# Maxima of a masked attention over pieces of 512, 512, 512 and 65 columns instead of four of about 401

## The reference

```python
scores = scale * einsum("bhqd,bhkd->bhqk", q, k)      # 2048 x 1601 a head
scores = where(mask, -large, scores)                  # int32 mask, 2048 x 1601
out    = softmax(scores) @ v                          # then the output projection
```

## Time and profile before

| | before |
|---|---|
| median of 3 runs | 3051.54 us (3050.11 to 3053.46) |
| the profiled execution's own time | 3052.74 us |
| its span | 3051.0 us |
| PE busy | 2817.6 us, 92% |
| DVE busy | 2171.2 us, 71% |
| ACT busy | 1824.3 us, 60% |
| POOL busy | 542.7 us, 18% |
| TensorE clock granted, mean over the span | 0.952 |

### The profile page before, as it was taken

How to read it: one execution, slowest core, us unless ns; L and a number is a source line. 1 busy time by engine, 2 the same in 40 slices (tenths; PEclk the granted TensorE clock), 3 DMA queues, 4 the chain that set the end, 5 groups by cost and what they waited for, 6 DMA issues and landing times. The chain is left out here.

```text
span 3051.0 us, 93944 instructions
## 1 busy us (share of the span) xinstructions
PE 2817.6 (92%) x39186; PEld 1046.2 (34%) x39187; DVE 2171.2 (71%) x6062; ACT 1824.3 (60%) x2158; POOL 542.7 (18%) x760
## 2 busy tenths in 40 slices
PE   4999999999999999967999998999999999899997
PEld 2522222522222222233222224652222222256664
DVE  7688986587878887565899993158888888652114
ACT  2388878436666666734588886234777777831222
POOL 0188870110000000001222113111000000002330
PEclk7899999979999999978899999997999999999999
DMA  3345541301110001102111112020111111111112
GB/s 98 111 130 131 135 111 35 118 18 25 25 26 25 17 24 26 36 20 76 33 47 43 42 45 83 1 74 23 39 52 52 52 53 32 35 58 62 44 43 86
DMA packets 120407, 166.79 MB, mean 55 GB/s; under 512 B 38227, under 2 KB 89310, under 8 KB 119984
## 3 DMA queue, kind: packets, MB, share of 16 engines
q1 hardware_dynamic: 102192, 117.21, 14.3%
q0 software_dynamic: 12320, 43.02, 4.6%
q10 hardware_dynamic: 5472, 0.56, 0.2%
HBM read 126.51 MB, written 26.72 MB: 50 GB/s over the span
## 5 line engine op out<-in xcount | busy, mean ns | idle before, releaser
L737 DVE TENSOR_REDUCE mpart<-ps 128x1 f32<-128x512 f32 (+2 forms) x1792 | 1014.2, 616 | 149.2 <-PE ps L548 148.1
L548 PE MATMUL ps<-stack 48*32 48x401 f16 (+5 forms) x13312 | 987.9, 355 | 55.3 <-DVE mpart L737 25.3
L475 ACT ACTIVATE xT<-ps,exp_scale 128x1024 f32<-128x1024 f32 (+3 forms) x800 | 794.6, 1028 | 284.6 <-PE ps L569 137.5
L475 ACT ACTIVATE cn<-ps,exp_scale 128x1024 f32<-128x1024 f32 (+4 forms) x800 | 743.1, 959 | 233.6 <-PE ps L569 119.7
L569 PE MATMUL ps<-stack 50*32 50x512 f16 (+3 forms) x11648 | 744.4, 377 | 56.2 <-ACT xT L475 42.3
L548 PEld LDWEIGHTS ps<-stack 48*32 48x32 f16 x13312 | 293.3, 91 | 1056.6 <-DVE mpart L737 562.8
L733 DVE CUSTOM_DVE_ANT_0 scrap<-ps,arena 128x401 bf16<-128x401 f32 (+1 forms) x1024 | 534.3, 574 | 128.0 <-PE ps L548 128.0
L609 PE MATMUL ps<-xT,vall 128*17 128x512 f32 (+4 forms) x3648 | 422.5, 524 | 2.2 <-POOL xT L434 1.4
L609 PE MATMUL ps<-cn,vall 128*17 128x512 f32 (+3 forms) x3392 | 412.9, 508 | 1.0 <-ACT cn L475 1.0
L569 PEld LDWEIGHTS ps<-stack 50*32 50x32 f16 x11648 | 194.6, 91 | 209.2 <-ACT xT L475 110.5
L727 DVE CUSTOM_DVE_ANT_0 scrap<-ps,scrap 128x128 bf16<-128x128 f32 (+3 forms) x512 | 247.6, 485 | 19.7 <-PE ps L548 15.1
(11 more groups left out here) (281 smaller groups left out, 2510.9 us busy)
## 6 DMA issues: line engine op xcount, KB each, us to landing
stack<-q_parts SPq DMA_DIRECT2D x384, 64.0 KB, 2.6
stack<-k_parts SPq DMA_DIRECT2D x192, 64.0 KB, 2.9
wbuf<-in_maskT POOLq DMA_DIRECT2D x24, 512.0 KB, 4.7
arena<-in_moe_w SPq DMA_DIRECT2D x19, 512.0 KB, 4.4
stack<-k_parts SPq DMA_DIRECT2D x192, 50.0 KB, 2.3
stack<-sums_inverse SPq DMA_DIRECT2D x16, 512.0 KB, 5.6
parts<-osb SPq DMA_DIRECT2D x240, 32.0 KB
wbuf<-in_mask POOLq DMA_DIRECT2D x16, 401.0 KB, 4.0
```

The source lines that it names most:

```text
L475: nc.scalar.activation(e.prob[tile % P_SLOTS][0:rows, half * HALF + first:(half + 1) * HALF], S_PS(g)[0:rows, first:HALF], ACT.Exp, scale= ...
L548: last = nc.tensor.matmul(bank[quarter(j), 0:w], qs[b][rows, t * P + 32 * j:t * P + 32 * j + 32], ks[b][rows, a:a + w], start=True, stop=True)
L737: nc.vector.tensor_reduce(dst, src, AX, ALU.max).then_inc(unit_used, 1)
```

## The change

Two lines. In the masked attention the 1601 keys are cut at `CH = 512` columns, where they were cut into four pieces of 401, 401, 401 and 398. The other attentions are cut as before. And `LEAST_UP` is 1 where it was 2^-9, so a weight is divided by a power of two that is at least 1.

```diff
-LEAST_UP = 2.0 ** -9
+LEAST_UP = 1.0
...
-        cut = tiles((t + 1) * P, CH) if causal else tiles(keys, -(-keys // -(-keys // CH)))
+        cut = tiles((t + 1) * P, CH) if causal else tiles(keys, CH if masked else -(-keys // -(-keys // CH)))
```

## The result

| | before | changed |
|---|---|---|
| median | 3052.26 us (3050.11 to 3053.46, 4 runs) | 3083.07 us (3075.15 to 3086.89, 4 runs) |
| the profiled execution's own time | 3052.74 us | 3086.89 us |
| its span | 3051.0 us | 3085.1 us |
| first reduction to first mask matmul (front) | 42.4 us | 43.7 us |
| first to last mask matmul (ring) | 664.7 us | 690.5 us |

The ratio is 1.0097, with a 95% interval of 1.0083 to 1.0111, or 25 to 34 us. The median of before has one run more than the one in the first table. The lower rows of the table are read from the first and last starts of L733 and L587 in the two traces.

The account below looks back on a forecast made before the run. Taken as bound: PE in the masked attention's ring, with DVE's two reductions on the path in each pair of five, and DVE in the front. Ring +22.9 and front +2 made +25, 3077 us for the median, range 3065 to 3085.

Parts of the forecast that it names:

- DVE's two reductions are the path in every pair of five: Ring: matmul of a, DVE a, DVE b, matmul of e are the path, in both patterns.
- pair of five: Ring: two steps, from product to product, with five units a to e; twelve a head, beside one of four.
- +0.31 in six pairs of a head, -0.29 in the other seven together: Ring: six pairs have a, b both 512 wide, +0.31 us each; other seven, -0.29 for all; sum +1.57 a head.
- 14.6 heads, +22.9: Ring: units stand in heads 0 to 13 and some 0.6 of head 14; 14.6 x 1.57 = +22.9 us.
- The front, +2: Before the ring, 85 units behind DVE: stalls of 0.06 twice a tile, 1.9 us for 16 tiles, +2 us.
- Prices: Masked attention: DVE starts 0.61 us apart at 512 columns, 0.14 at 65; a 512-wide matmul 46 ns longer than 401-wide.
- The sum, +25: Whole kernel: ring +22.9 and front +2 give +25 us, 3077 for the median.
- Matmuls of the two halves of the array pass each other: Ring, on PE: additions let each array half run by itself; strict program order would give heads of 42.9, +20 us.
- nothing moves: Rival, whole kernel: 3052 us, both engines' totals equal and DVE 25% idle; chance 0.05.
- columns alone: Rival, ring: e's wait mostly off the path, only growth of two-unit stretches left, +9, 3061 us; chance 0.08.
- faster: Rival, ring: short piece empties a bank early, the 0.09 wait vanishes everywhere, -16 with +9, 3044 us; chance 0.03.
- more: Rival, ring and front: 65-wide reduction near 0.20, low clock into ring, seven pairs save nothing, 3088 us; chance 0.04.

Follow-up runs that it names:

- e4: Against the kernel before: matmuls as before (401, 401, 401, 398), but DVE reduces 512, 512, 512 and 65 columns; 3069.46 us, ratio 1.0045.
- e5: Against the kernel before: a table of widths, narrow pieces for units first and second behind a product, wide ones elsewhere; 3037.33 us, ratio 0.9939.
- e7: Against e5: the same 64 widths, first two pieces of each tile exchanged with the last two; 3073.79 us, ratio 1.0077 to the kernel before.

## Why the prediction was right, step by step

- *DVE's two reductions are the path in every pair of five.* Shown for the pairs where it decides: with DVE's width alone (e4) all six grow by 0.22 to 0.23, which is two reductions of 0.115 more, and the two placings (e5, e7) agree. "Every" goes too far. In the first pair of a head ACT copies the head's output before its next exponentials, and the scores wait for them; that pair keeps its length in e4. From the trace of the kernel before:

```profile
987.46 0.11 PEld L569 LDWEIGHTS ps<-stack 50*32 50x32 f16 x8 [0.48 <-ACT xT L475]
```

  In the changed kernel DVE is on the path in the six pairs, and in the other seven it no longer is.
- *+0.31 in six pairs of a head, -0.29 in the other seven together.* In the head that the earlier trace rows belong to, the distances between mask blocks in the two traces give for the six pairs +0.315 to +0.321, together 1.91 (1.86 forecast), and for the seven -0.31 (-0.29). Single ones of the seven lie between -0.24 and +0.09. A head grew by 1.60, and 1.57 was the sum. From a to the mask block behind e it is 2.14 in each of the six and 1.85 in the pair of 1031.09 below, where b is 65 wide. One remark of the prediction is loose: of the 0.27 by which e comes later, 0.05 is the wider matmul of a, and the wait itself went from 0.09 to 0.27 (0.47 behind d, where 0.20 would do).
- *14.6 heads, +22.9.* The cut alone has a ring 23.0 us longer than before.
- *The front, +2.* It was +1.3 (and it has 83 units by the kernel's own count, 64 and 19, not 85). The step that was too large is the stall: DVE stops once a tile and not twice. From the front of the changed kernel, DVE's timeline:

```profile
619.75 0.69 DVE L733 CUSTOM_DVE_ANT_0 scrap<-ps,arena 128x512 bf16<-128x512 f32 x1
...
620.36 0.23 DVE L733 CUSTOM_DVE_ANT_0 scrap<-ps,arena 128x65 bf16<-128x65 f32 x1
620.50 0.08 DVE L733 DVE_READ_ACCUMULATOR2_ANT mpart<- 128x1 f32 x1
620.55 0.69 DVE L733 CUSTOM_DVE_ANT_0 scrap<-ps,arena 128x512 bf16<-128x512 f32 x1
```

  The reduction behind the 65-wide one comes 0.19 after it, where 0.14 would do without a wait; the others follow each other by 0.61, with no stall. A tile took 2.03 (620.55 to 622.59), 0.05 more than before.
- *Prices.* 0.61 between starts for 512 columns (1014.57 to 1015.19), 0.14 to 0.15 for 65 (1012.87 to 1013.01 in the same timeline), 46 ns more for a matmul: as taken.
- *The sum, +25.* The median is 31 above that of before, and 25 is at the lower end of the interval (25.3). Ring and front account for 24.3 in the profile of the cut alone. The changed kernel's profile has 27.1 there, because the low TensorE clock of the front (1.2 GHz) lasted on: it is still granted from 648 to 657 us, at the start of the ring, and only then the high one (columns as the earlier trace rows):

```profile
648.00:657.00 9.00, 9.00 (x108) 1.49 (x100) 3.69 (x15) 4.45 (x4) 6.18 (x10) 0.50 0.16 37
657.00:670.00 13.00, 12.84 (x236) 3.42 (x220) 9.76 (x39) 8.10 (x8) 4.83 (x8) 0.98 0.01 2
```

  In the cut alone, whose ring begins 1 us earlier, the high clock came back within the first of these stretches:

```profile
647.00:656.00 9.00, 9.00 (x156) 2.05 (x140) 5.89 (x24) 5.93 (x6) 6.14 (x9) 0.84 0.14 35
```

  The first head took 45.4 in the changed kernel and 42.7 in the cut alone, which has the same instructions in this place and differs in `LEAST_UP` only. The rest of the changed kernel's longer span lies in phases that the change doesn't touch; behind the ring the ten profiles have 1737 to 1748 us, the scale alone the most and the exchanged table the least, before 1740.5. What decides this, and with it the last few us between 3077, 3081 and 3083, stays open; the interval holds 3081 and 3083, and 3077 is at its lower end. So the sum is borne out for ring and front; of the 6 us by which the median lies above it, the profile puts 2.8 on the clock, and the others are not explained.
- *Matmuls of the two halves of the array pass each other.* The additions that let each half run by itself gave heads of 43.8, and these were measured; with a strict order on PE they gave less loss than was seen and too long a head before. No run tested it by itself, but the traces show it. Scores behind a unit, in the changed kernel:

```profile
1031.09 0.40 PE L548 MATMUL ps<-stack 48*32 48x512 f16 x4
1031.12 0.59 PE L569 MATMUL ps<-stack 50*32 50x512 f16 x8
...
1032.94 0.61 PE L587 MATMUL ps<-arena,big 128*32 128x512 fp8e4 x8
```

  Scores start 0.03 after the unit, as in the earlier trace rows. Their eight matmuls are two fours, and the second four came 0.15 behind the first with a 401-wide unit and 0.20 with this one: one half waits for the unit to stream its columns, the other doesn't. Which four is which shows in the unmasked attention of the kernel before, where the eighth of the program's order, on the lower rows, raises a semaphore. Of the 286 groups of eight from 2150 to 2600 us whose records are complete, it is among the first four to start in 118.
- The rivals: nothing moves, columns alone and faster fell with the result and with e4; "more" (3088) was nearer in its time than in its reasons. The seven pairs did save what was forecast, and the 65-wide reduction had no price of 0.20; of its reasons only the low clock in the ring came, in the changed kernel's profile.

## What to carry to other kernels

Equal totals on two engines don't make two cuts equal: where a few buffers go round, it matters which pieces stand right behind a long stretch without any. The consumer starts on them late and their buffers are wanted back first, and that set the price here. Give these the small pieces and put the large ones where the consumer has time; with the places known when the program is written, a table of widths did this at no instruction, -0.6% of the whole kernel by one attention. Before judging such a cut, follow one buffer through the timeline: producer, consumer, release, next producer.

## What the runs showed of the hardware

- A reduction with accumulator read lasts 226, 575 and 688 ns for 65, 401 and 512 columns, but the next one starts after 0.14, 0.50 and 0.61 us: some 0.08 of a reduction lies under the next, down to 65 columns.
- A bank goes from the end of DVE's read to PE's weights in 0.05 to 0.06 us (1015.88 to 1015.93), and from the end of PE's matmuls to DVE in 0.05 (1014.52 to 1014.57). PE's change between half rows and all rows takes 0.10 to 0.11 us behind the last column (e's weights at 1015.93, 0.21 for its columns, the mask block at 1016.26).
- Score matmuls on one half of the array's rows start ahead of earlier ones on the other half (118 of 286 groups in the unmasked attention, see above).
- With the same instructions in the same place, the low clock lasted longer in the changed kernel's profiled execution than in that of the cut alone, which was worth 2.8 us of the ring (690.5 against 687.7), all of it in the first head. Their `LEAST_UP` differs; why the low clock lasted longer is open.
